# Cross attention on one core: value products in fp32 instead of three in fp16, and scores of two units as two 64-row products side by side

## The reference, cut to what matters

```python
Q = proj(query, Wq, bq)
K = proj(key, Wk, bk)
V = proj(value, Wv, bv)
scores = jnp.einsum('bhqd,bhkd->bhqk', Q, K) / np.sqrt(D_K)
m = mask[:, None, :, :]
scores = jnp.where(m == 0, NEG, scores)
attn = jax.nn.softmax(scores, axis=-1)
x = jnp.einsum('bhqk,bhkd->bhqd', attn, V)
```

## Time and profile before

| what | us |
|---|---|
| median of 3 runs | 1293.64 |
| lowest, highest | 1292.46, 1300.71 |
| the profiled execution | 1291.09 |
| its span, first to last instruction | 1289.3 |
| PE busy in the span | 1087.8 (84%) |
| DVE busy | 961.6 (75%) |
| ACT busy | 704.9 (55%) |
| POOL busy | 388.9 (30%) |

### The profile page before, as it was taken

One profiled execution on the slowest core, in us unless ns is written; L12 is line 12 of the kernel. 1 busy time (PEld: TensorE's weight loads), 2 busy tenths in 40 slices (PEclk: granted clock), 3 DMA queues, 4 the chain that ended last, 5 costly groups with the idle time before them and its releaser, 6 DMA issues. The chain is left out here.

```text
span 1289.3 us, 30260 instructions
## 1 busy us (share of the span) xinstructions
PE 1087.8 (84%) x10763; PEld 881.4 (68%) x10763; DVE 961.6 (75%) x2254; ACT 704.9 (55%) x1459; POOL 388.9 (30%) x538
## 2 busy tenths in 40 slices
PE   4899989999987699986269999389999569999696
PEld 3578878778776577774257777378787447777485
DVE  7587877878875488884938883569998538888497
ACT  2454444444443355552637775368788525655484
POOL 5122222222220355551130000423331225555232
PEclk9899999999999799995559999699999879999799
DMA  6000000100000500005245431300000000000011
GB/s 257 5 10 2 10 12 2 71 3 2 2 2 2 187 23 22 11 9 227 107 135 172 171 108 49 120 17 26 24 9 9 0 24 23 11 21 9 34 50 50
DMA packets 34072, 65.35 MB, mean 51 GB/s; under 512 B 7590, under 2 KB 23334, under 8 KB 30886
## 3 DMA queue, kind: packets, MB, share of 16 engines
q1 hardware_dynamic: 32422, 59.62, 13.2%
q0 software_dynamic: 1536, 4.20, 1.0%
HBM read 43.03 MB, written 12.39 MB: 43 GB/s over the span
## 5 line engine op out<-in xcount | busy, mean ns | idle before, releaser
L953 POOL TENSOR_TENSOR ca_z<-ca_z,ca_top 128x308 f32<-128x308 f32 x128 | 92.7, 724 | 129.8 <-DVE ca_top L1082 129.5
L389 ACT ACTIVATE wa_probs<-wa_scores,wa_minus_top 128x192 f32<-128x192 f32 x256 | 83.3, 437 | 80.6 <-DVE wa_minus_top L477 80.6
L1025 ACT ACTIVATE ca_pth<-ca_turned 77x512 f16<-77x512 f32 x128 | 75.9, 593 | 59.0 <-PE ca_turned L1209 58.4
L348 POOL TENSOR_TENSOR wa_q<-wa_by_cos,wa_by_sin 128x256 f32<-128x256 f32 x32 | 23.4, 732 | 266.3 <-DVE wa_by_sin L472 266.3
L1209 PE MATMUL ca_turned<-ident,ca_probs 128*77 128x128 f32 x512 | 84.1, 287 | 20.6 <-ACT ca_probs L1017 19.5
L400 ACT ACTIVATE wa_pth<-wa_turned 128x384 f16<-128x384 f32 x128 | 58.4, 506 | 73.5 <-PE wa_turned L696 73.5
L1200 PE MATMUL ca_scores<-ca_km,ca_q 128*128 128x308 f32 x256 | 89.6, 433 | 6.0 <-ACT ca_q L998 5.7
L1087 DVE SCALAR_TENSOR_TENSOR ca_ptl<-ca_turned,ca_pth 77x512 f16<-77x512 f32 x128 | 86.7, 677 | 2.6 <-ACT ca_pth L1025 2.6
L1017 ACT ACTIVATE ca_probs<-ca_z 128x308 f32<-128x308 f32 x128 | 58.2, 455 | 44.8 <-POOL ca_z L953 43.8
L621 PE MATMUL wa_scores<-wa_xh,wa_wh 128*128 128x256 f16 x256 | 70.5, 275 | 11.7 <-DVE wa_wl L456 9.7
L477 DVE TENSOR_REDUCE wa_minus_top<-wa_scores 128x2 f32<-128x384 f32 x128 | 62.3, 549 | 21.1 <-PE wa_scores L684 18.9
(11 more groups left out here) (332 smaller groups left out, 3677.0 us busy)
## 6 DMA issues: line engine op xcount, KB each, us to landing
ex_stage<-in_ew SPq DMA_DIRECT2D x16, 1024.0 KB, 7.0
slots<-slots_zeros SPq DMA_DIRECT2D x10, 512.0 KB, 5.3
ca_xs<-tokens SPq DMA_DIRECT2D x16, 256.0 KB, 2.3
ex_xe<-slots SPq DMA_DIRECT2D x11, 320.0 KB, 3.3
slots<-ex_y SPq DMA_DIRECT2D x9, 320.0 KB
wa_x_stage<-in_xt SPq DMA_DIRECT2D x8, 256.0 KB, 3.0
tokens<-in_x SPq DMA_DIRECT2D x1, 2048.0 KB, 14.8
ca_w<-in_xw SPq DMA_DIRECT2D x2, 1024.0 KB, 5.6
```

Source lines behind the costliest of these rows:

```text
L389: ins = act.activation(probs[2 * (u % 2) + t][:, h, t * WINDOW:t * WINDOW + SPAN], s_bank[i][:, t * SPAN:(t + 1) * SPAN], ACT.Exp, bias=mi ...
L953: pool.tensor_tensor(z[k][:], z[k][:], top[:, k].unsqueeze(2).broadcast_to((P, UH, CTX)), ALU.subtract).then_inc(shift, 1)
L1025: act.activation(pth[k][0:CTX], t_bank[k][0:CTX], ACT.Copy, scale=PSCALE).then_inc(probs_high, 1)
```

## The change

Two things, in both cross attentions.

**Values in fp32.** ACT copies the transposed probabilities into one fp32 buffer pt (77 x 512), and the value projection is kept as one fp32 tensor v with the constant 1 in its 17th column. `weigh` makes one fp32 product per head. `probs_rest`, `value_high`, `value_low` and the tensors vh, vl, pth, ptl are gone.

**Scores in pairs.** `score_pair` runs at every even c. It makes the scores of units c+2 and c+3, which are two halves of the same 128 partitions of q: partitions 0 to 63 with the four heads of the first unit, 64 to 127 with those of the second, each into its own PSUM bank. It waits for both banks' masks and signals once, after the second product.

The diff, cut to its core:

```diff
@@ ACT
-                    act.activation(pth[k][0:CTX], t_bank[k][0:CTX], ACT.Copy, scale=PSCALE).then_inc(probs_high, 1)
+                    act.activation(pt[k][0:CTX], t_bank[k][0:CTX], ACT.Copy).then_inc(probs_kept, 1)
...
-                    if c == 2 and after:
-                        value_high(b + 1, 1 - par)
@@ DVE
-                dve.wait_ge(scores, b * UNITS + c + 1)
+                dve.wait_ge(scores, b * (UNITS // 2) + c // 2 + 1)
...
-            def probs_rest(b, c):
-                k = c % 2
-                dve.wait_ge(probs_high, b * UNITS + c + 1)
-                dve.scalar_tensor_tensor(out=ptl[k][0:CTX], in0=t_bank[k][0:CTX], scalar=PSCALE, in1=pth[k][0:CTX],
-                                         op0=ALU.mult, op1=ALU.subtract).then_inc(probs_low, 1)
...
                         mask_scores(*two_on)
-                    probs_rest(b, c)
-                    if two_on:
                         take_maximum(*two_on)
@@ PE
-            def score(b, c, par):
+            def score_pair(b, c, par):
                 t, part = divmod(c, UNITS // TPB)
-                g, h = part // 2, UH * (part % 2)
+                g = part // 2
...
-                if not (first(b) and c < 2):
-                    pe.wait_ge(masked, b * UNITS + c - 1)
-                pe.matmul(s_bank[c % 2][:, 0:UH * CTX], q[par][:, g, t * P:(t + 1) * P],
-                          km[par][:, g, h:h + UH].rearrange("p h k -> p (h k)"), start=True, stop=True).then_inc(scores, 1)
+                if not (first(b) and c == 0):
+                    pe.wait_ge(masked, b * UNITS + c)
+                for k in range(2):
+                    rows = slice(HALF * k, HALF * (k + 1))
+                    ins = pe.matmul(s_bank[k][:, 0:UH * CTX], q[par][rows, g, t * P:(t + 1) * P],
+                                    km[par][rows, g, UH * k:UH * (k + 1)].rearrange("p h k -> p (h k)"), start=True, stop=True)
+                ins.then_inc(scores, 1)
...
-                    cols = slice(h * P, (h + 1) * P)
-                    for n, (a, x) in enumerate(((pth[k], vh[par]), (pth[k], vl[par]), (ptl[k], vh[par]))):
-                        ins = pe.matmul(o_bank[t][:, head, 0:CD + 1], a[0:CTX, cols], x[0:CTX, head],
-                                        start=(n == 0), stop=(n == 2))
+                    ins = pe.matmul(o_bank[t][:, head, 0:CD + 1], pt[k][0:CTX, h * P:(h + 1) * P], v[par][0:CTX, head],
+                                    start=True, stop=True)
...
                     turn_probs(b, c)
-                    if c < UNITS - 2:
-                        score(b, c + 2, par)
-                    elif after:
-                        score(b + 1, c + 2 - UNITS, 1 - par)
+                    if c % 2 == 0:
+                        if c < UNITS - 2:
+                            score_pair(b, c + 2, par)
+                        elif after:
+                            score_pair(b + 1, 0, 1 - par)
```

More of the change, by code:

```diff
@@ L774 @@
 UH = 4
+HALF = UH * CD
 UNITS = TPB * CH // UH
@@ L835, in cross_attention @@
         km = [sb(f"km{k}", [P, KT_, CH // KT_, CTX]) for k in range(2)]
-        v = sb("v", [P, CH, CD])
-        vh = [sb(f"vh{k}", [P, CH, CD + 1], F16) for k in range(2)]
-        vl = [sb(f"vl{k}", [P, CH, CD + 1], F16) for k in range(2)]
+        v = [sb(f"v{k}", [P, CH, CD + 1]) for k in range(2)]
         z = [sb(f"z{k}", [P, UH, CTX]) for k in range(2)]
@@ L841, in cross_attention @@
         probs = [sb(f"probs{k}", [P, UH, CTX]) for k in range(2)]
-        pth = [sb(f"pth{k}", [P, UH * P], F16) for k in range(2)]
-        ptl = [sb(f"ptl{k}", [P, UH * P], F16) for k in range(2)]
+        pt = [sb(f"pt{k}", [P, UH * P]) for k in range(2)]
         inv = sb("inv", [P, TPB, CH])
@@ L862, in cross_attention @@
         key_masked = sem("key_masked")
-        v_high = sem("v_high")
-        v_low = sem("v_low")
         token_sum = sem("token_sum")
@@ L871, in cross_attention @@
         probs_t = sem("probs_t")
-        probs_high = sem("probs_high")
-        probs_low = sem("probs_low")
+        probs_kept = sem("probs_kept")
         weighted = sem("weighted")
@@ L1006, in step @@
                 ins.then_inc(free[bank], 1)
-            def value_high(b, par):
-                wait_read(act, [("value", 0)], b)
-                act.activation(vh[par][0:CTX, :, 0:CD], v[0:CTX], ACT.Copy, scale=SCALE).then_inc(v_high, 1)
             def power(b, c):
@@ L1032, in batch @@
                         step(b + d, (par + d) % 2, kind, i, bank, uses)
-                    if c == 2 and after:
-                        value_high(b + 1, 1 - par)
-            act.wait_ge(ones, 1)
             for kind, i, bank, uses in CA.prologue():
                 step(0, 0, kind, i, bank, uses)
-            value_high(0, 0)
             power(0, 0)
@@ L1047, in _ @@
             for k in range(2):
-                dve.memset(vh[k][:, :, CD:CD + 1], SCALE)
-                ins = dve.memset(vl[k][:, :, CD:CD + 1], 0.0)
+                ins = dve.memset(v[k][:, :, CD:CD + 1], 1.0)
             ins.then_inc(ones, 1)
@@ L1054, in value @@
                 dve.wait_ge(full[bank], uses + 1)
-                if not first(b):
-                    dve.wait_ge(v_low, b)
-                dve.tensor_tensor(v[0:CTX], shared[bank][0:CTX, 0:DIM].rearrange("p (h d) -> p h d", h=CH),
+                dve.tensor_tensor(v[par][0:CTX, :, 0:CD], shared[bank][0:CTX, 0:DIM].rearrange("p (h d) -> p h d", h=CH),
                                   rows[0:CTX, 0].rearrange("p (h d) -> p h d", h=CH), ALU.add).then_inc(free[bank], 1)
[L1060 to L1063, removed]
             def mask_scores(b, c):
                 k = c % 2
-                dve.wait_ge(scores, b * UNITS + c + 1)
+                dve.wait_ge(scores, b * (UNITS // 2) + c // 2 + 1)
                 if not (first(b) and c < 2):
@@ L1128, in batch @@
                         norm.apply(dve, b - 1, 1, at(X, (b - 1) * TPB + 1))
-                    if c == 2 and after:
-                        value_low(b + 1, 1 - par)
             for kind, i, bank, uses in CA.prologue():
@@ L1134, in _ @@
                     value(0, 0, bank, uses)
-            value_low(0, 0)
             if not additive:
@@ L1206, in turn_probs @@
                 if not (first(b) and c < 2):
-                    pe.wait_ge(probs_low, b * UNITS + c - 1)
+                    pe.wait_ge(probs_kept, b * UNITS + c - 1)
                 for h in range(UH):
@@ L1213, in weigh @@
                 k, t = c % 2, c // (UNITS // TPB)
-                pe.wait_ge(probs_low, b * UNITS + c + 1)
+                pe.wait_ge(probs_kept, b * UNITS + c + 1)
                 if c == 0:
-                    pe.wait_ge(v_low, b + 1)
+                    wait_read(pe, [("value", 0)], b)
+                    if first(b):
+                        pe.wait_ge(ones, 1)
                 if c % (UNITS // TPB) == 0 and not first(b):
@@ L1244, in _ @@
                 step(0, 0, kind, i, bank, uses)
-            score(0, 0, 0)
-            score(0, 1, 0)
+            score_pair(0, 0, 0)
             both(batch)(pe)
```

## The result

The changed kernel takes 1320.2 us (median of 4 runs, 1318.2 to 1325.1) against 1293.2 (1292.5 to 1300.7) before: a ratio of 1.019, 95% interval 1.016 to 1.023: 27 us more by the medians, 25 by the ratio. The profiled execution took 1325.1 us with a span of 1323.3, 34.0 more than the span before.

The account below looks back on a forecast made before the run. PE (16.5 of 18.37 us a batch) and the loop through DVE share the bound, PE fuller. 16.5 + 4.0 - 0.5 plus 0.1 waiting gives 20.1 us a batch, +22 us in all, 1316 us; range 1299 to 1346.

Parts of the forecast that it names:

- 12 full batches: Steady batches of six to eight units' work in the cross attentions: 20.1 us each, +1.7 on 18.37, together +20.8 us.
- first batch of both attentions: Start of each cross attention: lacks the second heads and mix step (1.1 us), so +0.5 us each.
- last batch of both: End of each cross attention, no steps ahead: shorter loops against longer stretches and end, about 0.
- Values, +4.0 a batch: Value products on PE: eight fp32 records at 0.11 us, a unit 0.80 us instead of 0.31, +4.0 us a batch.
- Scores, -0.5 a batch: Score products on PE: a pair costs 0.52 + 0.40 for switching form instead of 1.04 us, -0.5 us a batch.
- rival 2: Score pairs on PE: the two halves don't overlap, a pair takes 1.44 us, +29, 1345 us; 10 in 100.
- Rival 1: PE: switches and loads cheaper than their rows, or slack takes the extra in; 1295 to 1306 us; 17 in 100.
- The new wait, 0: PE before a score pair waits for the mask of unit c+1; costed at nothing, bound 0.4 us a pair.
- Waits left, 0.1: PE's remaining waiting in a full batch: both loops covered, 0.1 us left, making 20.1 us a batch.
- DVE's relief: DVE without L1087 and the value splits: 4.8 us less a batch, and 0.4 for the splits.
- Rival 3: PE and DVE: fp32 weight loads hide behind other work and DVE was the real bound; 1247 us; 8 in 100.
- a rival over the full batches: PE's granted clock falls: pitches double at 1.2 GHz, one batch in four there costs some +70 us; 5 in 100.

Follow-up runs that it names:

- one-column kernel: The changed kernel with value products streaming 1 column instead of 17, so only the sum of the probabilities is made: 1306.7 and 1323.3 us in two runs.
- half the load: The changed kernel with value products of 64 weight columns instead of 128, half of each unit's tokens left out: 1303.7 us.
- the run with whole products: The changed kernel with both score products of a pair over all 128 partitions, order and waits kept: 1327.9 us, ratio 1.025.

## Why the prediction was right, and where its sizes were off

The forecast was 1316 us, slower by more than 1%, with PE as the only full engine; 1320.2 was measured. Of the profiled pair, the spans differ by 34.0 us:

| part | predicted | measured |
|---|---|---|
| 12 full batches | +20.8 | +19.1 |
| first batch of both attentions | +1.0 | +8.1 |
| last batch of both | 0 | +1.6 |
| the other stages | 0 | +5.2 |

The full batches are 12 x 1.59 (ten intervals of 19.93 against 18.34 on average). The attentions as a whole, from their first instruction to their last, grew by 14.0 and 14.8 us; what the full batches and the tails do not hold is the first batch's. The tails, from the last value addition to the end, grew by 1.9 and 2.1 us, of which 1.2 each are three quarters of a full batch. The stages that nobody touched differ by 5.2 us. Over the other profiled executions they take from 950 to 959 us (the one-column kernel aside), so 5.2 lies within the scatter; the profiled execution of the changed kernel is 4.9 us above its median and that of the kernel before 2.2 below. That 1316 came so near 1320 is in part luck: the full batches came out below the forecast and the rest above it.

**Values, +4.0 a batch.** Right. The records stand 0.112 apart, a unit takes 0.81 us, forecast 0.80; (0.81 - 0.31) x 8 = 4.0. Both bounds were rows at 77 columns and at 1 column, and both said 0.11; the runs with half the load and with one column show that this is the load.

**Scores, -0.5 a batch.** Right in kind, a little small: 0.70 by the run with whole products. The halves overlap (rival 2 falls), the second records come 0.36 later, which holds the load on the way in, 0.10 as counted, and there is a bare gap of some 0.1 on each side. The step that was too dear is the load behind the pair: 0.06 shows, where 0.11 was counted. That makes 0.35 a pair instead of 0.40. Rival 1, a free switch, falls too: at -2.1 a batch the beat would be 18.5. The Trainium skill (TensorEngine Tiling (Array Packing), Theoretical Speedup) offers up to 2x for 64 rows; a pair here runs 1.04 / 0.87 = 1.2 times as fast. The bare gap on each side agrees with the drain that the Trainium skill names on the same page (Key Properties); the two bare loads, 0.16, come on top.

**The new wait, 0.** Right for this kernel, for a reason that the forecast gave (a relieved DVE): 20.63 with pairs in order, 20.64 without. With fp16 values the order in pairs costs 1.5 us a batch, but there too PE has no wait for a mask; it waits for the exponential.

**Waits left, 0.1.** They are 0.0. The beat is 19.93 for a forecast of 20.1: 0.2 of the scores' term and 0.1 of waits, less 0.1 elsewhere.

**DVE's relief.** Forecast were 4.8 us of DVE a batch, and 0.4 for the value split; its busy time fell by 3.8 (15.8 to 12.1). The forecast took off the 0.60 from L1087 to the maximum, but left out that the maximum then stands 0.52 behind its mask, where L1087 stood 0.39 behind it. It changed nothing in the time, as PE was the fuller engine. Rival 3 (1247 us) needed loads under 0.08; they are 0.112.

**First and last batches, +1.0.** This is the term that was sized wrongly: +9.7 in the profiled pair. The forecast priced the first batch by its work at the full clock, and counted the clock only as a rival over the full batches (5 in 100), where it stays at 1.00. At the start of the attentions, where PE waits for its inputs, the granted clock stood at 1.2 GHz for 42 us in the changed kernel's profile and for 21 in that of the kernel before. With both starts filled it is 14 and 17, and the attentions differ by 18.9 us instead of 28.8, which is no more than the full batches. So the clock accounts for the difference at the start in this pair. How much of it belongs to the change, and how much to the execution that was profiled, stays open: by the ratios, filling takes 6 us from the changed kernel and 4 to 5 from the one before, which is the same within the noise.

**Sums.** Two figures of the forecast don't follow from its terms: rival 1's batch of 18.5 us makes 1294 us over 14 batches, not 1296, and the top of the range is 1330, not 1332. Neither changes a reading.

## What to carry to other kernels

An fp32 product with few streamed columns costs its two weight loads, 0.11 us for each 128 columns, so three fp16 products at 0.025 us each are cheaper on PE than one in fp32; the DVE work that the fp32 form saves, worth at most 1.3 us a batch here, did not pay for 4.0 on PE. Count PE's pitches first. A single pair of 64-row products gives back little: entry and exit take 0.35 of the 0.52 us that it could save. And price the first batch of a stage apart from the steady one, since its clock is open: between 7 and 24 us at 1.2 GHz in the attentions here. A few products put into the idle start gave 0.3 to 0.8% in four kernels; what a kernel gains there has to be measured against the same kernel unfilled.

## What was not expected of the hardware

A PE that the trace shows busy for 17.10 of 17.10 us can stay at 1.2 GHz all that time, with fp32 value products whose time is the weight load; it then went to 2.4 GHz in the same kind of batch. The runs here don't tell what decided it. It came in one attention of two in the changed kernel and in the one-column kernel, in neither with fp32 values alone, with whole products or with half the load, in neither of the filled kernel's, and in no kernel with fp16 values. A product with 64 weight columns instead of 128 cost a change of form as one with 64 rows does, 0.10 us in and 0.10 out, though nothing ran beside it.
